# Second attention of a two-block transformer: probabilities in two buffers, transposes four units behind the scores, one PSUM bank alone for the products with V

## The reference, cut to what matters

```python
k = jnp.concatenate([k_p, k_r], axis=-1)
q = jnp.concatenate([q_p, q_r], axis=-1)
scores = jnp.einsum('bqhd,bkhd->bhqk', q, k) * scale
scores = jnp.where(causal[None, None], scores, jnp.finfo(scores.dtype).min)
probs = jax.nn.softmax(scores, axis=-1)
out = jnp.einsum('bhqk,bkhd->bqhd', probs, v).reshape(b, s, H)
return out @ o_w
```

## Time and profile before

| | |
|---|---|
| median of 3 runs | 2243.07 us (2238.32 to 2246.05) |
| the profiled execution | 2245.4 us, its span 2243.7 us |
| mean granted TensorE clock | 0.861 |
| TensorE matmul busy | 1938.5 us, 86% |
| VectorE, ScalarE, GpSimd busy | 1362.5, 958.5, 768.0 us |
| scores L805, transposes and their kin L821 | 157.4 us (512 records), 134.8 us (640) |

### The profile page before, as it was taken

How to read it: one execution, slowest core, us unless ns; L and a number is a source line. 1 busy time by engine, 2 the same in 40 slices (tenths; PEclk the granted TensorE clock), 3 DMA queues, 4 the chain that set the end, 5 groups by cost and what they waited for, 6 DMA issues and landing times. The chain is left out here.

```text
span 2243.7 us, 24181 instructions
## 1 busy us (share of the span) xinstructions
PE 1938.5 (86%) x8266; PEld 1131.3 (50%) x8266; DVE 1362.5 (61%) x1988; ACT 958.5 (43%) x1942; POOL 768.0 (34%) x669
## 2 busy tenths in 40 slices
PE   7887666887999898987999898987899899898796
PEld 3455444444457565543447555544446665544442
DVE  6765896444564798654554699554554599564311
ACT  1412872441322895442232696342142498243022
POOL 1255483331210376332120176342120157343201
PEclk9999756767999999767999999868899999956798
DMA  6347000000213283200123175200022167300483
GB/s 250 113 134 241 0 0 19 1 1 0 94 43 113 87 274 131 91 20 1 42 81 124 34 254 185 113 19 1 10 107 91 52 217 233 122 20 1 191 312 116
DMA packets 55048, 220.79 MB, mean 98 GB/s; under 512 B 6288, under 2 KB 6288, under 8 KB 46992
## 3 DMA queue, kind: packets, MB, share of 16 engines
q1 hardware_dynamic: 45776, 195.14, 24.9%
q0 software_dynamic: 5120, 16.78, 2.0%
q10 hardware_dynamic: 4032, 7.34, 0.9%
HBM read 179.65 MB, written 39.58 MB: 98 GB/s over the span
## 5 line engine op out<-in xcount | busy, mean ns | idle before, releaser
L1958 POOL TENSOR_TENSOR Y<-Y,HC 128x1024 f32<-128x1024 f32 x116 | 273.7, 2360 | 174.2 <-DVE HC L1341 173.5
L1330 DVE TENSOR_TENSOR_SCAN HS<-DA,ps 128x1024 f32<-128x1024 f32 x128 | 292.2, 2284 | 23.5 <-PE ps L717 13.1
L1896 POOL TENSOR_TENSOR PD<-PD,RDN 128x1024 f32<-128x1024 f32 (+3 forms) x128 | 164.0, 1293 | 336.0 <-DVE RDN L1526 335.9
L1842 ACT ACTIVATE PD<-ps,NMX 128x512 f32<-128x512 f32 (+3 forms) x256 | 131.9, 524 | 232.9 <-PE ps L821 200.4
L1707 ACT ACTIVATE DA<-DL,AB,AN 128x511 f32<-128x511 f32 x256 | 193.8, 806 | 14.7 <-DVE HS L1330 13.5
L509 PE MATMUL ps<-ring,XNT 128*128 128x512 f32 x384 | 186.4, 645 | 12.9 <-PEq L1991 8.6
L1517 DVE TENSOR_REDUCE NMX<-ps 128x2 f32<-128x1024 f32 (+3 forms) x128 | 102.2, 819 | 149.6 <-PE ps L808 149.1
L805 PE MATMUL ps<-KT,QT 32*128 32x128 f32 (+3 forms) x512 | 157.4, 704 | 36.4 <-ACT AOTD L1826 32.4
L982 PE MATMUL ps<-ring,XBT 128*128 128x512 f32 x384 | 187.0, 593 | 0.0
L821 PE MATMUL ps<-pack,PD 128*128 128x128 f32 x640 | 134.8, 363 | 16.1 <-ACT PTD L865 12.7
L625 PE MATMUL ps<-XNH,tern 128*128 128x512 f32 x352 | 139.2, 395 | 9.7 <-DVE tern L1230 5.4
(11 more groups left out here) (244 smaller groups left out, 3792.9 us busy)
## 6 DMA issues: line engine op xcount, KB each, us to landing
ring<-experts_dram SPq DMA_DIRECT2D x48, 1024.0 KB, 5.1
tern<-tern_q SPq DMA_DIRECT2D x33, 768.0 KB, 4.2
ring<-experts_dram SPq DMA_DIRECT2D x48, 512.0 KB, 5.4
RAW<-tern_dram SPq DMA_DIRECT2D x22, 768.0 KB, 4.8
ring<-wqkv_dram SPq DMA_DIRECT2D x4, 3072.0 KB, 14.2
XB<-xg SPq DMA_DIRECT2D x42, 256.0 KB, 3.5
yg<-YB SPq DMA_DIRECT2D x42, 256.0 KB, 4.9
tern_q<-tern SPq DMA_DIRECT2D x11, 768.0 KB, 7.1
```

The source lines that it names most:

```text
L1330: v.tensor_tensor_scan(HS[:, q].rearrange("p j t -> p (j t)"), DA[:, q].rearrange("p j t -> p (j t)"), ps[:, 2 * q:2 * q + 2].rearrange("p ...
L1842: ins = s.activation(probs(places[x])[:, 0:n], ps[:, bank, col:col + n], ACT.Exp, bias=NMX[:, p % 2, c:c + 1], accum_out=DEN[:, p % 2, c:c ...
L1896: ins = p.tensor_tensor(both, both, RDN[:, pair % 2, c:c + 2].rearrange("p (x o) -> p x o", o=1) .to_broadcast([P, 2, n]), ALU.mult)
L1958: p.tensor_tensor(y, y, HC[:, q], ALU.add).then_inc(c_y, 1)
```

## The change

`PD` gets a second set of buffers (`PD2` in `arena`, `PD3` in `tern`), used by odd pairs, so the exponentials of unit k wait for T(k-6). DEPTH becomes 4. The units m = 2 put both heads into bank 6, 256 columns each; bank 7 holds PV alone, and the wait of the scores for `d_head` is gone. As the two heads of such a unit now write one bank, they don't run side by side: the first head's scores and mask, then T(k-4) (with PV where it is due), then a wait for the first (`d_first`), then the second head's. PV(g) moves from behind S(6g+9) to behind S(6g+10), its copy by ScalarE with it. The second part of the projection moves from k = 25 to k = 26.

```diff
-DEPTH = 3
+DEPTH = 4
...
-        yield i, n, [(x, 2 + 2 * m + x, col) for x in range(2)]
+        yield i, n, [(x, 2 + 2 * m + x, col) if m < 2 else (x, 6, x * n) for x in range(2)]
...
-    PD = (at("PD0", [P, 4, T], F32, "v1"), at("PD1", [P, T], F32, "tern", 8 * KB))
+    PD = ((at("PD0", [P, 4, T], F32, "v1"), at("PD1", [P, T], F32, "tern", 8 * KB)),
+          (at("PD2", [P, 4, T], F32, "arena"), at("PD3", [P, T], F32, "tern", 10 * KB)))
...
             for k in range(NU + DEPTH + 1):
+
+                def turn():
+                    if k >= 6 + DEPTH and (k - DEPTH) % 6 == 0:
+                        pe_D_pv(pe, (k - DEPTH) // 6 - 1)
+                    if DEPTH <= k < NU + DEPTH:
+                        pe_D_turn(pe, k - DEPTH)
+
                 if k < NU:
-                    pe_D_scores(pe, k)
-                if k >= 9 and k % 6 == 3:
-                    pe_D_pv(pe, k // 6 - 1)
-                if DEPTH <= k < NU + DEPTH:
-                    pe_D_turn(pe, k - DEPTH)
+                    pe_D_scores(pe, k, turn)
+                else:
+                    turn()
                 if k in NEXT_AT:
                     pe_norm(pe, 0, NEXT_AT[k])
-                if k in (NU, NU + 1):
+                if k in (NU, NU + 2):
                     pe_D_project(pe, (0, 1) if k == NU else (2, 3))
...
-        def pe_D_scores(pe, k):
+        def pe_D_scores(pe, k, turn):
...
-            if k >= 11 and k % 6 == 5:
-                pe.wait_ge(d_head, k // 6)
...
+            if k % len(D_TILES) < 2:
...
+                last.then_inc(d_scores, 1)
+                turn()
+                return
+
+            (i, n, places), = d_parts(k)
+            for x, ((h, rows), (_, bank, col)) in enumerate(zip(heads_of(p), places)):
+                if x:
+                    turn()
+                    pe.wait_ge(d_first, p + 1)
+                scores(i, n, h, rows, bank, col)
+                mask(n, bank, col).then_inc(d_scores if x else d_first, 1)
...
-            pe.wait_ge(d_exp, min(6 * g + 9, NU))
...
-                if k >= 10 and k % 6 == 4:
-                    g = k // 6 - 1
+                if k >= 7 + DEPTH and (k - 1 - DEPTH) % 6 == 0:
+                    g = (k - 1 - DEPTH) // 6 - 1
                     s.wait_ge(d_pv, g + 1)
                     s.copy(AOTD[:, g], ps[:, 7]).then_inc(d_head, 1)
...
-            if k >= DEPTH:
-                s.wait_ge(t_full, T_INDEX["p", k - DEPTH, 1] + 1)
+            if k >= 6:
+                s.wait_ge(t_full, T_INDEX["p", k - 6, 1] + 1)
```

More of the change, by code:

```diff
@@ L384, in build @@
         d_scores = sem("d_scores")
+        d_first = sem("d_first")
         d_max = sem("d_max")
@@ L800, in pe_D_scores, with scores, mask @@
                 pe.wait_ge(d_exp, k - len(D_TILES) + 1)
-            if k >= 11 and k % 6 == 5:
-                pe.wait_ge(d_head, k // 6)
-            for i, n, places in d_parts(k):
-                for (h, rows), (_, bank, col) in zip(heads_of(p), places):
-                    pe.matmul(ps[:, bank, col:col + n], QT[rows, h // 4, tile(i)], KT[rows, h // 4, 0:n],
-                              start=True, stop=False, skip_group_check=True)
-                for _, bank, col in places:
-                    last = pe.matmul(ps[:, bank, col + n - P:col + n], identb, mask_q, start=False, stop=True,
-                                     skip_group_check=True)
-            last.then_inc(d_scores, 1)
+            def scores(i, n, h, rows, bank, col):
+                pe.matmul(ps[:, bank, col:col + n], QT[rows, h // 4, tile(i)], KT[rows, h // 4, 0:n],
+                          start=True, stop=False, skip_group_check=True)
+            def mask(n, bank, col):
+                return pe.matmul(ps[:, bank, col + n - P:col + n], identb, mask_q, start=False, stop=True,
+                                 skip_group_check=True)
+            if k % len(D_TILES) < 2:
+                for i, n, places in d_parts(k):
+                    for (h, rows), (_, bank, col) in zip(heads_of(p), places):
+                        scores(i, n, h, rows, bank, col)
+                    for _, bank, col in places:
+                        last = mask(n, bank, col)
+                last.then_inc(d_scores, 1)
[6 more added lines that the diff above has]
+                    pe.wait_ge(d_first, p + 1)
+                scores(i, n, h, rows, bank, col)
+                mask(n, bank, col).then_inc(d_scores if x else d_first, 1)
         def pe_D_turn(pe, k):
@@ L820, in pe_D_turn @@
                         place = at + (i - kt if x else kt) * P
-                        last = pe.transpose(ps[:, bank, place:place + P], probs(places[x])[:, tile(kt)], ident)
+                        last = pe.transpose(ps[:, bank, place:place + P], probs(k // len(D_TILES), places[x])[:, tile(kt)], ident)
                 last.then_inc(t_full, 1)
@@ L847, in pe_D_project, with probs @@
                               skip_group_check=True)
-        def probs(place):
-            x, bank, col = place
-            return PD[1][:, x * (T // 2):] if bank >= 6 else PD[0][:, bank - 2, col:]
+        def probs(p, place):
+            _, bank, col = place
+            wide, narrow = PD[p % 2]
+            return narrow[:, col:] if bank == 6 else wide[:, bank - 2, col:]
         def copy_p(eng, copy, k, x):
@@ L1516, in v_D_max @@
                 c = d_column(i, 0)
-                ins = v.tensor_reduce(NMX[:, p % 2, c:c + 2], ps[:, bank:bank + 2, col:col + n], AX.X, ALU.max, negate=True)
+                src = (ps[:, 6].rearrange("p (x n) -> p x n", x=2) if m == 2 else ps[:, bank:bank + 2, col:col + n])
+                ins = v.tensor_reduce(NMX[:, p % 2, c:c + 2], src, AX.X, ALU.max, negate=True)
             ins.then_inc(d_max, 1)
@@ L1841, in s_D_exp @@
                     c = d_column(i, x)
-                    ins = s.activation(probs(places[x])[:, 0:n], ps[:, bank, col:col + n], ACT.Exp,
+                    ins = s.activation(probs(p, places[x])[:, 0:n], ps[:, bank, col:col + n], ACT.Exp,
                                        bias=NMX[:, p % 2, c:c + 1], accum_out=DEN[:, p % 2, c:c + 1])
@@ L1892, in p_D_scale @@
                 _, bank, col = places[0]
-                both = (PD[1][:].rearrange("p (x n) -> p x n", x=2) if m == 2
-                        else PD[0][:, bank - 2:bank, col:col + n])
+                wide, narrow = PD[pair % 2]
+                both = narrow[:].rearrange("p (x n) -> p x n", x=2) if m == 2 else wide[:, bank - 2:bank, col:col + n]
                 c = d_column(i, 0)
```

## The result

The change makes the kernel slower: **2258.59 us** (median, 2258.25 to 2260.49) against 2243.07, a ratio of 1.0074 (95% interval 1.0045 to 1.0104). The forecast was 2230 us with a range up to 2248, so the time lies outside it.

A forecast was written before the change was run, and what follows sets the result against it. TensorE's own list was taken to set the pace. Terms of -3.6 - 6.6 + 5.1 + 2.4 - 0.7 + 0.2 gave -3.2 us per loop, -13 in all: median 2230 us, range 2196 to 2248.

The forecast's parts named there:

- The chain of ScalarE's copies: Maxima, exponentials, copy behind each unit's scores: 3.0, 3.8, 2.3 us; no wait at half clock, some at full.
- the half-clock pair: Sign: a pair of heads' scores and transposes at half clock would take 12.1 to 12.3 us.
- items 1, 4 and 5: Short transposes' waits go, -3.6 us a loop; norms at k = 14, 20 wait, +2.4; start -0.7, drain +0.2.
- item 2: Behind the three PVs: waits for PV's bank go, early work at full clock comes; -6.6 us a loop.
- item 3: Heads of m = 2 no longer side by side: 1.16 us a unit at half clock, +5.1 us a loop.
- early work at full clock: Behind PV, scores and transposes run at full clock where waits for PV's bank stood; part of -6.6 us a loop.
- the slower rival: Thinner scores lose the clock: fast stretches behind PV end about 3 us early; about 2258 us; chance 0.13.
- The clock stays up: Rival: full clock could last from first PV to projection; 2197 us, partly so 2205 to 2215; chance 0.20.
- the one that the prediction weighed: Skill's sentence: continuous matmul work brings full clock, longer idle gaps lose it; by that rule 2168 us.

The follow-up runs named there:

- h2: g1 with the other head's scores, read by nobody, computed beside each half at k = 11, 17, 23; 2210.62 us, 0.9848 of the kernel before.
- g4: f1 with the four norm transposes ahead of T(k-4) in bank 1, their copy first; 2171.55 us, 0.9647 of the kernel before.
- g1: f1 with only units k = 11, 17 and 23 divided, each head in its own bank; 2207.63 us, 0.9808 of the kernel before.
- i2: The change with scores nobody reads put ahead of T(8), T(14) and T(20), where TensorE waits; 2244.77 us, 0.9995 of the kernel before.
- h1: f1 with all eight m = 2 units a loop divided, each head in its own bank; 2254.62 us, 1.0042 of the kernel before.
- e3: The kernel before with only the heads of m = 2 units taken apart in time, each in its own bank; 2302.93 us, 1.0254.
- f1: The change without the division: second buffers, DEPTH 4, early copy of PV's bank, heads side by side; 2176.88 us, 0.9689 of the kernel before.
- f2: f1 with DEPTH 3 instead of 4; 2203.71 us, 0.9808 of the kernel before.

## Why the prediction was wrong

**Right, by its own steps.** The waits went where it said: `d_head` none, the short transposes none in half-clock pairs, the start's gone. New waits were T(8) 0.33 and 0.37 (forecast 0.8 together), T(14) the same (0.8), norm 14 1.60 (1.6), norm 16 0.77 (0.65), norm 20 2.46 (2.3), T(20) 1.60 and 0.36 (2.0). The chain of ScalarE's copies holds. The mean clock stayed at 0.62 (forecast 0.61 to 0.68). Of its other signs, the half-clock pair took 12.46 us (12.1 to 12.3), and the loops 108.1 to 108.5 (near 105).

**Where the 26 us between forecast and result lie.** In the terms of the account. The forecast's idle time is what items 1, 4 and 5 sum to and, in item 2, waits of 3.4, 4.1 and 3.4 us less new ones of 0.8, 1.45 and 2.0: -8.35 us a loop. Its work is eight second heads at 1.16. What is left to its -3.2 us is work moved to full clock, 4.1 us a loop: 3.4 in item 2 and 0.7 for unit 2 in item 3. Four times that:

| four loops, us | idle | work | busy at full | length |
|---|---|---|---|---|
| the forecast | -33 | +37 | +16 | -13 |
| measured | -26.3 | +42.4 | +3.3 | +12.8 |

**The step that failed is the clock outside the stretches behind PV.** The forecast changed it nowhere, and counted unit 2's second head as full-clock work in every loop (item 3). The "early work at full clock" of item 2 itself came, and more: 20 us behind the PVs, forecast 14. But at the loops' starts 5 us of full-clock work went (forecast 3 more), and all 12 us of the stray stretches. All places together, full-clock work fell 13 us short of the forecast, half of the 26. The starts are accident: full clock there lasted 7.0 us in the first loop of before, 2.8, 4.2 and 2.8 in the others, and 2.3 to 2.7 in the change; I took the first loop for all four. Of the stray stretches I knew nothing, as the earlier trace rows shows two loops; the others, in the same columns, say how far the clock of like loops ranges in one execution, 0.61 to 0.68:

```profile
922.44:1030.09 107.65, 91.07 (x453) 48.63 (x453) 62.92 (x109) 47.58 (x163) 43.71 (x40) 0.62 0.03 11
...
1960.11:2070.20 110.09, 93.89 (x452) 48.98 (x453) 63.00 (x109) 47.58 (x163) 43.71 (x40) 0.61 0.03 10
```

The experiments suggest that the stray stretches go with the division (seven kernels of eight); the reason is open.

**A wait put at nothing.** The norm at k = 18 waits 1.61 us in the first loop and 2.07 in the other three, before 0.36: 6.4 us, nearly all of the 7 us of idle time that did not go. It has become the same case as k = 14, which I had priced.

**A size off.** Item 3 took 1.16 us a unit, under its stated upper end of 1.42; 1.27 was measured in the half-clock pair, the whole row again and next to nothing for the mask, and all work grew by 42.4 us for 37 forecast: the remaining 5. I argued that a row "shows mostly a dependence on columns", from 2.08 and 1.22; the direct reading, one head costs what two side by side cost, was there as the upper bound and was nearly right. The Trainium skill (TensorE: Matmul & The Clock Gate, Part 3, on packing small matmuls) says that small products in distinct row groups run concurrently; the trace agrees, 1.22 us for four records and 1.22 for two.

**Missed, and smaller.** Unit 2 runs at half clock (1.22 at 407.39). The projection starts at half clock for 3.4 us, before for 1.0: its twelve records ahead of the next transposes take 7.11 us, before 5.81. TensorE's timeline of before, and of the change:

```profile
511.24 5.81 PE L846 MATMUL ps<-pack,AOTD 128*128 128x512 f32 x12
```

```profile
512.08 7.11 PE L867 MATMUL ps<-pack,AOTD 128*128 128x512 f32 x12
```

**The rivals.** The time came where the slower rival had it (2258), but by luck, not by its mechanism: the fast stretches behind PV are 6.8, 10.2 and 6.8 us a loop, before 6.8 each, so none ended early; and full density (h2) leaves them as they are. "The clock stays up" has substance in kernels with fewer divided units or none: g4's loops run at 0.71 to 0.77, g1's at 0.69 to 0.75. There the Trainium skill (TensorE: Matmul & The Clock Gate, Part 1, on depth-cycling of the PSUM queue) has a sentence that bears on the case better than the one that the prediction weighed: frequent micro-idles between groups of products make the clock swing between its levels. The trace agrees in part only: with such idles filled three stretches of eight were longer, and in i2's second loop the clock fell after 6.83 us without any.

**What stays open**: what decides whether a stretch at full clock lasts 6.8 or 13.7 us behind the same rows, and whether a stray one comes at all. Two rivals to the waits were not tested by a run: the point of the list at which the clock rises, by which the table above sorts, and the kind of work in a stretch, transposes against scores. Open, too, are the 0.3 points between h1 and the change.

## What to carry to other kernels

Products that share the array side by side are one product's price for two: before taking them apart to free a bank, look whether the bank's reader can come earlier in its own engine's list. Here that took 1.4% off the kernel before, new waits included, where the division added 3.5 points. Where the clock swings, split the trace's busy time by the granted clock, look where in the loop the full-clock time lies, and forecast idle, work and busy time at full clock each by itself, over all repetitions of the loop: the first loop of this kernel was not like the others. Price each wait of a kind at each place it can occur, the norm at 18 as well as at 14.

## What the runs showed that was not expected

Filling 0.7 us of waits with products nobody reads shortened the changed kernel by 0.8 points, and the following scores went from 1.65 to 0.91 us. Costs did not add up as their rows do: the division in time alone (e3) was 32 units at 1.36 us, 44 us, and took 57. In f1 dividing 12 of the units took 27 us and dividing the other 20 took 33, all 32 together 79. Depth 4, which I had priced as a cost, gave 1.2 points between f2 and f1. And a second head beside the first costs nothing: four float32 records of 32x256 for two heads took 1.22 us at half clock and 0.70 at full, two for one head took 1.22 and 0.69.
